# Transposes and first up parts of the first expert tile made inside the last attention iteration, and its first gelu part behind the squares of o

## The chip, the cores and the metric

One core of one Trainium2 chip. The metric is the device time of one execution in microseconds (us), lower is better. Engines: PE (TensorE, matmuls and their weight loads), VectorE (DVE in rows), ScalarE (ACT), GpSimd (POOL), and SyncE (SP), which only issues DMAs. The first four each run their own program in order; they meet at semaphores.

## The reference

A transformer layer in two halves, on x of 8 x 512 tokens by 256, f32.

```python
x = x + attention(layernorm(x))      # delta-rule linear attention, 4 heads, keys 128, values 64
x = x + experts(layernorm(x))        # top 2 of 8 experts, hidden 1024, exact gelu

# attention, for each token in order
pred = k_t^T S;  S = S + k_t (beta_t * (v_t - pred))^T;  o_t = q_t^T S
o = o * rsqrt(mean(o * o) + eps) * norm_w * silu(g);  return o @ Wo
# experts
out += w[:, eid] * (gelu(x @ w1[eid].T) @ w2[eid].T)
```

## The kernel before

The 4096 tokens are 32 tiles of 128 (T = 32). The **attention stage** is a software pipeline: in each iteration `i` of each engine's loop stand steps of several tiles in different states (PE `first_w(i - 3)`, `wo_make(i - 4)`, `xn2T_make(i - 5)`). The recurrence over a tile is solved as a triangular system: an inverse made in 7 levels (`y_make`, `x_make`), then `first_w`, `residual_make` and `corrected_w`, then the output (`out_state`, `out_chunk`). PE runs this loop for T + 3 iterations (L1483 to L1519). ScalarE and VectorE have their last iterations written out by hand, L1059 to L1136 and L2277 to L2359. The order of all work is that of the program text of each engine; no planner is at work.

A tile's last steps are a serial path over the engines: `out_chunk` (PE, L1392), `o_square` (ScalarE, L912, four squares with sums), `o_scale` (VectorE), `o_rsqrt` (GpSimd, L681), `o_norm` (VectorE, L1860), `oT_make` (PE, L1402), `oT_evac` (ScalarE) and `oT_low` (VectorE), `wo_make` (PE, L1416), `attention_residual` and `ln2_stats` (VectorE, L1869, L1876), `ln2_scale` (GpSimd, L628), `ln2` (ScalarE, L799), `xn2T_make` (PE, L1434), `xn2T_evac` (ScalarE, L929), `logits_make` (PE, L1448), `logits_copy` (ScalarE, L936), then the routing on VectorE (`best_logit` and what follows, every four tiles), ranks on PE (`rank`), and scattering of the rows into a table in HBM by GpSimd (`scatter`). Tokens of one expert stand together in that table.

In the same way a tile's W is made: `first_w` (PE, L1324), `first_w_evac` (ScalarE, L887), `residual_make` (PE, L1338), `residual` (VectorE, L1824), `corrected_w` (PE, L1356), `w_evac` (ScalarE, L895), `out_chunk`.

The **expert stage** takes 36 tiles of up to 256 rows, each belonging to one expert (8 of them to two). Tile 0 holds rows of the first 20 attention tiles, so it can be loaded while the last attention tiles are still worked on: SyncE's `load_rows(0, 0)` (L559, L569) reads 256 rows as soon as the table of experts is made. Steps of an expert tile: `xT_make` transposes its rows in four f32 transposes (PE, L1521, in rows L1533); `xT_hi` copies them to f16 (ScalarE, L1038) and `xT_lo` makes the rest that f16 leaves out (VectorE, L2228, in rows L2230); `up` (PE, L1557) makes hidden rows in 8 parts m of 6 matmuls each (products with high and low parts), raising `s_hps` after every second m; `hidden` (ScalarE, L1045) makes a gelu over two parts and its f16 copy; `hidden_lo` (VectorE, L2232) the low part of it; `down` (PE, L1577) the output product; `rows_out` and `accumulate` add the rows to the output. Every call of `up` reads the number of the expert into a register. ScalarE needs another table for gelu than for the functions of the attention stage; it is loaded by an instruction of its own that the compiler sets ahead of the gelu (a row ACT_TABLE_LOAD).

Matmuls of f16 stand in rows as L1158, copies on ScalarE as L789 and most small VectorE steps as L1901, since helpers make them; they are told apart by tile names. W is `first_w_evac`'s result, W_s `w_evac`'s, rho the residual's, rowA the normalised rows, w_hi and w_lo the up weights, w_s the down weights, osq the squares and o.

Around the change, PE before: last loop iteration (i = 34) with `wo_make(30)`, `rank(27)`, `first_w(31)`, `out_state(31)`, `residual_make(31)`, `corrected_w(31)`; then L1598 to L1632: `xT_make(0, 0)`, `out_chunk(31)`, `xn2T_make(30)`, `up(0, 0)` m 0 and 1, `logits_make(30)`, `up` m 2 and 3, `xT_make(0, 1)`, `oT_make(31)`, `up` m 4 and 5, `wo_make(31)`, and so on to `down(0, 0)`. ScalarE before (L1114 to L1130): `x_evac(31, 6)`, `first_w_evac(31)`, `late_hi(4)`, `late_hi(5)`, `w_evac(31)`, `ln2(30)`, `xT_hi(0, 0)`, `o_square(31)`, `xn2T_evac(30)`, `logits_copy(30)`, `late_hi(6)`, `xT_hi(0, 1)`, `oT_evac(31)`, `hidden` part 0. VectorE before (L2310 to L2331): `first_gate(27)`, `attention_residual(30)`, `ln2_stats(30)`, `residual(31)`, four routing steps, `xT_lo(0, 0)`, `o_scale(31)`, `o_norm(31)`.

Of the kernel before, what the change touches and what calls it, by code (L numbers as in the profile page):

```python
# [8 lines left out]
T = B * N // P  # L9
# [36 lines left out]
EARLY = 2 * T - LATE  # L46
# [25 lines left out]
def build(nc, x, wq, wk, wvg, wb, wo, norm_w, router, w1, w2, eye, fconst, iconst, out):  # L72
# [3 lines left out]
    with ctx:  # L76
# [210 lines left out]
        s_whi = sem("w_hi_ready")  # L287
# [499 lines left out]
        def _(act):  # L787
# [79 lines left out]
            def x_evac(n, lev):  # L867
                if not 0 <= n < T:
                    return
                q = n % 2  # L870
                done(act, s_xps[q], n // 2, 6, lev)
                if lev == LEVELS - 1:
                    evac(odd(XT[:, n % RING, :, :], lev), packed(p_xt[q], lev)).then_inc(s_xup[q], 1)
                    return
                evac(changed(n % RING, lev), PS[q][:, :].rearrange("p (w n s) -> p w n s", w=2, s=1 << lev)).then_inc(s_xup[q], 1)
# [11 lines left out]
            def first_w_evac(n):  # L887
                if not 0 <= n < T:
                    return

                done(act, s_zps, n - 1)
                done(act, s_wps, n)
                evac(W0[:, :, :], p_p).then_inc(s_ws, 1)
# [18 lines left out]
            def o_square(n):  # L912
                if not 0 <= n < T:
                    return
                done(act, s_oTp, n - 1)
                done(act, s_oarg, n - 1)
                done(act, s_ops, n)
                for h in range(H):
                    act.activation(osq[:, h, :], p_o[:, h, :], ACT.Square, scale=1.0 / O_SCALE,
                                   accum_out=osum[:, h:h + 1]).then_inc(s_osq, 1)  # L920
# [8 lines left out]
            def xn2T_evac(n):  # L929
                if not 0 <= n < T:  # L930
                    return
                done(act, s_lgps, n - 1)
                done(act, s_xn2Tp, n)
                evac(xn2T[:, :, :].rearrange("p k n -> p (k n)"), p_xn2T).then_inc(s_xn2Ts, 1)
# [103 lines left out]
            def xT_hi(i, q):  # L1038
                act.wait_ge(s_gTp, i * 4 + (q + 1))

                if not (isinstance(i, int) and i * 4 + q < 2):
                    act.wait_ge(s_hps, i * 16 + 4 * (q - 1))
                evac(xTh[:, q % 2, :, :], p_gT).then_inc(s_gTh, 1)

            def hidden(i, q, ms=range(4)):  # L1045
                for m in ms:
                    act.wait_ge(s_hps, i * 16 + (4 * q + m + 1))

                    if not (isinstance(i, int) and i * 4 + q < 1):
                        act.wait_ge(s_hlo, i * 16 + (4 * (q - 1) + m + 1))  # L1050
                    if m == 0 and not (isinstance(i, int) and i * 4 + q < 2):
                        act.wait_ge(s_yops, i * 4 + (q - 1))
                    n = halves(i, q) * P
                    gelu = hf[:, m, :].rearrange("p (m n) -> p m n", m=2)[:, :, 0:n]
                    act.activation(gelu, p_h[m].rearrange("p (m n) -> p m n", m=2)[:, :, 0:n], ACT.Gelu, scale=1.0 / W_SCALE).then_inc(s_gelu, 1)  # L1055
                    act.wait_ge(s_gelu, i * 16 + (4 * q + m + 1))
                    evac(hhi[:, q % 2, 2 * m:2 * m + 2, 0:n], gelu, H_SCALE).then_inc(s_hhi, 1)
# [54 lines left out]
            logits_copy(T - 3)  # L1112
            oT_evac(T - 2)
            x_evac(T - 1, 6)  # L1114
            first_w_evac(T - 1)
            late_hi(4)
            late_hi(5)

            w_evac(T - 1)
            ln2(T - 2)  # L1120
            xT_hi(0, 0)
            o_square(T - 1)
            xn2T_evac(T - 2)
            logits_copy(T - 2)
            late_hi(6)
            xT_hi(0, 1)
            oT_evac(T - 1)
            hidden(0, 0, range(0, 1))
            late_hi(7)
            hidden(0, 0, range(1, 2))  # L1130

# [24 lines left out]
        def _(pe):  # L1156
# [105 lines left out]
            def gram(n, a):  # L1262
                if not 0 <= n < T:
                    return
                for s in (s_kTs, s_kTl, s_qs, s_ql):
                    done(pe, s, n)

                if a == 1:
                    reach(pe, s_pos, Ranked.n)
                done(pe, s_AT, n - 1)  # L1270
                for h in range(2):
                    hh = [KQ[:, n % RING, part, 2 * a + h, :, :] for part in range(2)]
                    last = product(p_gram[a][:, h, :, :], [x[:, 0, :] for x in hh], hh)
                last.then_inc(s_gram, 1)
# [205 lines left out]
                Ranked.n = n // C + 1  # L1480

            pe.wait_ge(s_ident, 16)
            for i in range(T + 3):  # L1483
                gram(i - 2, 0)
                gram(i - 2, 1)
                out_chunk(i - 4)
                y_make(i - 3, 5)
                k_proj(i - 1, 0)
                xn2T_make(i - 5)
                y_make(i - 2, 0)  # L1490
                state_make(i - 4)
                x_make(i - 3, 5)
                y_make(i - 2, 1)
                logits_make(i - 5)
                k_proj(i - 1, 1)
                x_make(i - 2, 1)
                y_make(i - 3, 6)
                oT_make(i - 4)
                q_proj(i - 1, 0)
                y_make(i - 2, 2)  # L1500
                q_proj(i - 1, 1)
                beta_proj(i - 1)
                x_make(i - 3, 6)
                x_make(i - 2, 2)
                p_make(i - 2)
                wo_make(i - 4)
                y_make(i - 2, 3)
                rank(i - 7)
                first_w(i - 3)
                out_state(i - 3)  # L1510
                x_make(i - 2, 3)
                xnT_make(i)
                residual_make(i - 3)
                k_transposes(i - 1)
                y_make(i - 2, 4)
                vg_proj(i - 1, 0)
                vg_proj(i - 1, 1)
                corrected_w(i - 3)
                x_make(i - 2, 4)  # L1519

            def xT_make(i, q):  # L1521
                if isinstance(i, int):
                    i, q = divmod(i * 4 + q, 4)
# [71 lines left out]
                if KH - 1 in ms:  # L1595
                    last.then_inc(s_yops, 1)

            pe.wait_ge(s_xup[0], 6 * T // 2)  # L1598
            xT_make(0, 0)
            out_chunk(T - 1)  # L1600
            xn2T_make(T - 2)
            pe.wait_ge(s_tab, 1)
            pe.wait_ge(s_whi, EARLY)
            pe.wait_ge(s_wlo, EARLY)
            pe.wait_ge(s_xup[1], 6 * T // 2)
            up(0, 0, range(0, 2))
            logits_make(T - 2)
            done(pe, s_gs, T - 1)
            done(pe, s_th, T - 1)
# [72 lines left out]
        def _(dve):  # L1682
# [545 lines left out]
            def xT_lo(i, q):  # L2228
                dve.wait_ge(s_gTh, i * 4 + (q + 1))
                dve.tensor_tensor(xTl[:, q % 2, :, :], p_gT, xTh[:, q % 2, :, :], ALU.subtract).then_inc(s_gTl, 1)  # L2230
# [84 lines left out]
            oT_low(T - 2)  # L2315
            second_gate(T - 5)
            first_gate(T - 5)
            attention_residual(T - 2)
            ln2_stats(T - 2)
            residual(T - 1)  # L2320
# [2 lines left out]
            slot_sums(T - 5)  # L2323
            slots(T - 5)

            dve.wait_ge(s_xg[0], 16)
            xT_lo(0, 0)
            o_scale(T - 1)
            o_norm(T - 1)
            xT_lo(0, 1)  # L2330
# [118 lines left out]
```

## Time and profile before

| | |
|---|---|
| median of 3 runs | 910.33 us (907.74 to 911.69) |
| profiled execution, its own time | 914.49 us |
| its span | 912.7 us |
| PE busy | 850.3 us (93%) |
| VectorE, ScalarE, GpSimd busy | 625.5, 596.5, 439.3 us |
| mean granted PE clock | 0.978 of full |
| transition between the stages | about 480 to 512 us |

Times of rows are us from the start of the span. In a row of a timeline stand start, duration, engine, line, operation, output<-input, count, and in brackets the engine's idle time before it with what ended it. In a row of stretches stand, for each engine, the busy time and (in brackets) the count, then the granted clock of PE (1.00 is 2.4 GHz, 0.50 is 1.2 GHz), the share of the DMA engines at work, and GB/s. Consecutive matmuls overlap, so a duration is longer than the distance to the next start.

### The profile page before, as it was taken

Reading aid. Unit: us, or ns where it says so; the run is one execution under the profiler, and the core shown is the slowest. Engines: PE = TensorE matmul, PEld = TensorE weight load, DVE = VectorE, ACT = ScalarE, POOL = GpSimd, SP = SyncE. Lnnn points to the kernel's source line nnn. Section 1 sums busy time; section 2 is a strip of 40 time slices with the busy share of each in tenths; the row PEclk is TensorE's granted clock in tenths of the full one; section 3 lists DMA queues with packets and bytes.
Section 4 is the critical chain, followed back from the end, with each engine's and each line's share of the span. In section 5 each row is a group of like instructions: output and inputs, shape, how many; then the busy total and the mean of one; then the engine's idle time right before and its main releaser. Section 6 shows DMA issues by size and latency. Waiting matters only on the chain.

```text
span 912.7 us, 29508 instructions
## 1 busy us (share of the span) xinstructions
PE 850.3 (93%) x9870; PEld 669.4 (73%) x9871; DVE 625.5 (69%) x1832; ACT 596.5 (65%) x1645; POOL 439.3 (48%) x430
## 2 busy tenths in 40 slices
PE   3799999999999999999988979999999999999995
PEld 2578887788877888778876657777777777777773
DVE  4678898898988989888885755544455554455552
ACT  3478887888888888888766725444446544444551
POOL 2155554767677676676646543332223222222333
PEclk8999999999999999999997989999999999999998
DMA  6022222333233332332233252322233332223223
GB/s 225 2 71 66 82 65 77 95 95 106 84 95 99 90 107 83 97 99 82 84 107 88 72 118 48 48 48 48 43 48 66 50 50 46 46 46 46 47 36 34
DMA packets 50652, 67.14 MB, mean 74 GB/s; under 512 B 6464, under 2 KB 35008, under 8 KB 50528
## 3 DMA queue, kind: packets, MB, share of 16 engines
q1 hardware_dynamic: 36640, 46.46, 17.5%
q0 software_dynamic: 13344, 17.97, 11.5%
q8 instruction: 79, 1.29, 0.6%
q10 hardware_dynamic: 544, 1.05, 0.3%
q14 instruction: 45, 0.37, 0.1%
HBM read 41.84 MB, written 23.61 MB: 72 GB/s over the span
## 4 chain that ended last, share of the span: by engine, by line
PE 77%; issue 7%; ACT 4%; DVE 4%; POOL 4%; DMA 3%; SPq 0%; DVEq 0%; ACTq 0%; POOLq 0%
PE ps L1158 71%; DMA wst<-w 2%; PE ps L1247 2%; PE ps L1533 2%; ACT inverse_levels L789 1%; PE ps L1190 1%; PE ps L1413 1%; POOL kscale L616 1%; DVE inverse_levels L1815 1%; DMA wb_in<-wb 1%; POOL out L769 1%; POOL w_lo L665 0%; PE ps L1445 0%; ACT kq_wvg L844 0%; ACT Lh L789 0%
## 5 line engine op out<-in xcount | busy, mean ns | idle before, releaser
L789 ACT ACTIVATE inverse_levels<-ps 128x512 f16<-128x512 f32 (+1 forms) x324 | 163.0, 520 | 147.9 <-PE ps L1533 120.6
L769 POOL DMA_INDIRECT out<-inverse_levels,yidx x71 | 119.6, 1684 | 256.2 <-DVE inverse_levels L2273 194.6
L1158 PE MATMUL ps<-inverse_levels,w_hi 128*128 128x256 f16 (+1 forms) x1376 | 192.9, 255 | 1.9 <-issue 1.3
L2236 DVE SCALAR_TENSOR_TENSOR KpAT<-kq_wvg,inverse_levels 128x512 f16<-128x512 f32 (+1 forms) x144 | 98.5, 687 | 111.9 <-ACT inverse_levels L789 109.2
L1158 PE MATMUL ps<-inverse_levels,w_lo 128*128 128x256 f16 (+1 forms) x688 | 164.2, 255 | 0.0
L1158 PE MATMUL ps<-w_s,inverse_levels 128*128 x426 | 141.9, 379 | 6.5 <-issue 3.3
L1158 PEld LDWEIGHTS ps<-inverse_levels,w_hi 128*128 x1376 | 125.4, 98 | 15.7 <-issue 3.2
L1055 ACT ACTIVATE kq_wvg<-ps 128x512 f32<-128x512 f32 (+1 forms) x144 | 85.0, 590 | 67.0 <-PE ps L1158 51.1
L1158 PE MATMUL ps<-w_s,KpAT 128*128 x426 | 116.1, 273 | 1.0 <-issue 1.0
L789 ACT ACTIVATE inverse_levels<-kq_wvg 128x512 f16<-128x512 f32 (+1 forms) x144 | 89.8, 624 | 4.6
L1815 DVE CAST_PREDICATED inverse_levels<-mask_s,ps 128x256 f16<-128x256 int8 x192 | 82.1, 428 | 15.0 <-PE ps L1158 10.0
L616 POOL TENSOR_TENSOR kscale<-karg,fc 128x8 f32<-128x8 f32 x32 | 52.7, 1647 | 81.6 <-DVE karg L1745 81.6
L1158 PEld LDWEIGHTS ps<-w_s,inverse_levels 128*128 128x128 f16 x426 | 41.6, 98 | 53.9 <-issue 10.0
L1158 PE MATMUL ps<-wqk,inverse_levels 128*128 128x512 f16 (+1 forms) x263 | 78.1, 384 | 2.8 <-DVE inverse_levels L1714 2.3
L1158 PE MATMUL ps<-inverse_levels 128*128 128x64 f16 x1408 | 68.8, 193 | 9.3 <-DVE inverse_levels L1815 9.1
L2269 DVE TENSOR_SCALAR inverse_levels<-ps,gate 128x256 f32<-128x256 f32 x69 | 30.3, 479 | 68.8 <-PE ps L1158 68.5
L694 POOL DMA_INDIRECT routed_rows<-rowA,slot x64 | 67.7, 1057 | 18.4 <-issue 12.4
L1158 PE MATMUL ps<-kq_wvg,inverse_levels 128*128 128x512 f16 (+1 forms) x263 | 73.5, 387 | 1.8 <-issue 1.8
L1158 PEld LDWEIGHTS ps<-inverse_levels 128*128 128x128 f16 x1408 | 55.8, 99 | 22.1 <-DVE inverse_levels L1815 13.6
L1158 PE MATMUL ps<-inverse_levels,Lh 128*128 128x64 f16 x896 | 64.2, 194 | 8.3 <-ACT inverse_levels L789 4.6
L1158 PEld LDWEIGHTS ps<-inverse_levels,w_lo 128*128 x688 | 67.6, 98 | 5.5
L1158 PEld LDWEIGHTS ps<-inverse_levels,Lh 128*128 128x128 f16 x896 | 47.2, 100 | 20.2 <-ACT inverse_levels L789 10.7
(239 smaller groups left out, 1920.7 us busy)
## 6 DMA issues: line engine op xcount, KB each, us to landing
wst<-w SPq DMA_DIRECT2D x58, 256.0 KB, 2.8
inverse_levels<-eye SPq DMA_DIRECT2D x35, 256.0 KB, 5.2
x_s<-x SPq DMA_DIRECT2D x32, 128.0 KB
out<-x_s SPq DMA_DIRECT2D x32, 128.0 KB, 1.7
x_s<-routed_rows SPq DMA_DIRECT2D x7, 260.0 KB
Lh<-routed_rows SPq DMA_DIRECT2D x7, 260.0 KB
Vp<-routed_rows SPq DMA_DIRECT2D x7, 260.0 KB
rowA<-routed_rows SPq DMA_DIRECT2D x7, 260.0 KB
```

The source lines that it names most:

```text
L616: return pool.tensor_tensor(dst, src, half_neg[:, 0:n], ALU.pow)
L694: pool.indirect_dma_start(out=routed, out_offset=bass.IndirectOffsetOnAxis(ap=slot[:, g % 2, k, c:c + 1], axis=0), in_=rowA[:, g % RG * C ...
L769: pool.indirect_dma_start(out=out, out_offset=bass.IndirectOffsetOnAxis(ap=yidx[:, q, a:a + 1], axis=0), in_=yrow[:, q % 2, a, :], in_offs ...
L789: return act.activation(dst, src, ACT.Copy, scale=scale)
L1055: act.activation(gelu, p_h[m].rearrange("p (m n) -> p m n", m=2)[:, :, 0:n], ACT.Gelu, scale=1.0 / W_SCALE).then_inc(s_gelu, 1)
L1158: return pe.matmul(dst, lhsT, rhs, start=start, stop=stop, **kw)
L1190: last = pe.transpose(p_xnT[:, k * P:(k + 1) * P], xn[:, k * P:(k + 1) * P], ident)
L1247: last = pe.transpose(p_kT[:, h, :], Kp[:, n % RING, h, :], ident)
L1533: last = pe.transpose(p_gT[:, k, a * P:(a + 1) * P], xg[q % 4][:, a, k * P:(k + 1) * P], ident)
L1815: dve.copy_predicated(even(Y[:, lev - 1, :, :], lev), level_mask(lev, 0, H), packed(p_y[q], lev)).then_inc(s_ys[q], 1)
L2236: dve.scalar_tensor_tensor(hlo[:, q % 2, two, 0:n], hf[:, m, :].rearrange("p (m n) -> p m n", m=2)[:, :, 0:n], H_SCALE, hhi[:, q % 2, two, ...
L2269: step(dve.tensor_scalar(yrow[:, par, a, :], p_yo[a][:, 0, :], gate[:, par, a:a + 1], None, ALU.mult))
```

## The change

On PE `xT_make(0, 0)` and the first two up parts of tile 0 move from behind the loop into its last iteration (i = T + 2 = 34): the transposes go ahead of `first_w(31)`, part m = 0 ahead of `out_state(31)`, part m = 1 behind `residual_make(31)`. The waits of these steps move with them. The definitions of `xT_make`, `expert_of`, `load_experts`, `parts_of`, `up` and `down` move above the loop, unchanged. On ScalarE `xT_hi(0, 0)` moves ahead of `first_w_evac(31)`, and part 0 of the gelu of tile 0 (`hidden(0, 0, range(0, 1))`) moves right behind `o_square(31)`, ahead of `xn2T_evac(30)`. On VectorE `xT_lo(0, 0)` moves ahead of `attention_residual(30)`.

```diff
@@ ScalarE
             x_evac(T - 1, 6)
+            xT_hi(0, 0)
             first_w_evac(T - 1)
             late_hi(4)
             late_hi(5)
 
             w_evac(T - 1)
             ln2(T - 2)
-            xT_hi(0, 0)
             o_square(T - 1)
+            hidden(0, 0, range(0, 1))
             xn2T_evac(T - 2)
             logits_copy(T - 2)
             late_hi(6)
             xT_hi(0, 1)
             oT_evac(T - 1)
-            hidden(0, 0, range(0, 1))
             late_hi(7)
             hidden(0, 0, range(1, 2))
@@ PE, in the loop
                 rank(i - 7)
+                if i == T + 2:
+                    pe.wait_ge(s_xup[0], 6 * T // 2)
+                    xT_make(0, 0)
                 first_w(i - 3)
+                if i == T + 2:
+                    pe.wait_ge(s_tab, 1)
+                    pe.wait_ge(s_whi, EARLY)
+                    pe.wait_ge(s_wlo, EARLY)
+                    pe.wait_ge(s_xup[1], 6 * T // 2)
+                    up(0, 0, range(0, 1))
                 out_state(i - 3)
                 x_make(i - 2, 3)
                 xnT_make(i)
                 residual_make(i - 3)
+                if i == T + 2:
+                    up(0, 0, range(1, 2))
                 k_transposes(i - 1)
@@ PE, behind the loop
-            pe.wait_ge(s_xup[0], 6 * T // 2)
-            xT_make(0, 0)
             out_chunk(T - 1)
             xn2T_make(T - 2)
-            pe.wait_ge(s_tab, 1)
-            pe.wait_ge(s_whi, EARLY)
-            pe.wait_ge(s_wlo, EARLY)
-            pe.wait_ge(s_xup[1], 6 * T // 2)
-            up(0, 0, range(0, 2))
             logits_make(T - 2)
@@ VectorE
             second_gate(T - 5)
             first_gate(T - 5)
+            dve.wait_ge(s_xg[0], 16)
+            xT_lo(0, 0)
             attention_residual(T - 2)
             ln2_stats(T - 2)
             residual(T - 1)
...
             slots(T - 5)
 
-            dve.wait_ge(s_xg[0], 16)
-            xT_lo(0, 0)
             o_scale(T - 1)
```

## Rows read from the trace of the kernel before

**Rows 1.** Busy time by stretch: stretch, its length, engines, granted clock, DMA share, GB/s

```profile
473.60:477.00 3.40, 3.19 (x42) 2.82 (x43) 1.72 (x8) 1.01 (x3) 0.00 (x0) 0.51 0.28 108
477.00:480.40 3.40, 1.88 (x46) 1.52 (x44) 3.13 (x16) 2.57 (x6) 2.18 (x4) 0.99 0.02 5
480.40:490.60 10.20, 8.44 (x82) 6.90 (x79) 5.73 (x25) 5.53 (x20) 5.29 (x6) 0.51 0.24 65
490.60:494.00 3.40, 2.59 (x31) 2.05 (x28) 2.31 (x7) 3.00 (x8) 3.09 (x5) 0.98 0.30 74
...
486.50:487.50 1.00, 0.27 (x5) 0.11 (x3) 0.43 (x2) 0.66 (x2) 0.72 (x1) 0.50 0.00 0
700.00:880.00 180.00, 180.00 (x1398) 137.45 (x1397) 94.06 (x215) 91.41 (x151) 56.83 (x34) 1.00 0.31 48
```

**Rows 2.** Chain of work that ended last, in the transition

```profile
499.81 1.28 ACT L1055
...
507.99 0.19 ACT logits L789
```

**Rows 3.** Timeline of PE

```profile
487.64 1.44 PE L1158 MATMUL ps<-wo_s,inverse_levels 128*128 128x256 f16 x6 [0.87 <-DVE inverse_levels L1721]
...
489.13 0.37 PE L1158 MATMUL ps<-R,inverse_levels 128*128 128x64 f16 x4
489.32 0.83 PE L1158 MATMUL ps<-S_s,kq_wvg 128*128 128x64 f16 x12
490.24 0.21 PE L1158 MATMUL ps<-W,Lh 128*128 128x64 f16 x1
...
491.64 0.19 PE L1158 MATMUL ps<-rho,inverse_levels 128*128 128x64 f16 x1 [0.67 <-DVE rho L1829]
...
491.93 0.63 PE L1533 MATMUL ps<-fc,x_s 128*128 128x128 f32 x4
492.63 1.08 PE L1158 MATMUL ps<-W_s,KpAT 128*128 128x64 f32 x8
...
494.56 0.39 PE L1158 MATMUL ps<-inverse_levels,w_hi 128*128 128x256 f16 x2 [0.62 <-DVE inverse_levels L2230]
...
495.87 0.56 PE L1158 MATMUL ps<-router_s,inverse_levels 128*128 128x8 f32 x4
...
498.73 0.38 PE L1413 MATMUL ps<-fc,osq 128*128 128x128 f32 x2
...
512.22 0.39 PE L1158 MATMUL ps<-w_s,inverse_levels 128*128 x1 [0.72 <-DVE KpAT L2236]
...
534.65 1.06 PE L1533 MATMUL ps<-fc,x_s 128*128 128x128 f32 x4
```

**Rows 4.** Timeline of ScalarE

```profile
489.61 0.38 ACT L789 ACTIVATE W<-ps 128x256 f16<-128x256 f32 x1 [2.29 <-PE ps L1158]
...
492.93 0.59 ACT L789 ACTIVATE inverse_levels<-ps 128x512 f16<-128x512 f32 x1
493.83 0.22 ACT L919 ACTIVATE osq<-ps 128x64 f32<-128x64 f32 x1 [0.32 <-PE ps L1158]
...
494.63 0.40 ACT L789 ACTIVATE inverse_levels<-ps 128x256 f32<-128x256 f32 x1
...
499.81 1.28 ACT L1055 ACT_TABLE_LOAD   x1
...
502.28 0.61 ACT L789 ACTIVATE kq_wvg<-wst 128x512 f16<-128x512 f32 x1
```

**Rows 5.** Timeline of VectorE

```profile
491.07 0.42 DVE L1829 SCALAR_TENSOR_TENSOR rho<-Vp,ps 128x256 f16<-128x256 f32 x1 [0.67 <-PE ps L1158]
...
493.61 0.69 DVE L2230 TENSOR_TENSOR inverse_levels<-ps,inverse_levels 128x512 f16<-128x512 f32 x1 [0.49 <-ACT inverse_levels L789]
...
496.18 0.86 DVE L1865 SCALAR_TENSOR_TENSOR osq<-ps,ors,gs 128x64 f32<-128x64 f32 x4 [1.15 <-POOL ors L616]
```

**Rows 6.** Timeline of SyncE: the row load of expert tile 0

```profile
483.21 0.41 SPq L559 DMA_DIRECT2D x_s<-routed_rows  x1
```

More of the change, by code:

```diff
@@ L1482, in _ @@
             pe.wait_ge(s_ident, 16)
[L1483 to L1519, printed above, removed]
             def xT_make(i, q):
@@ L1596, in down @@
                     last.then_inc(s_yops, 1)
-            pe.wait_ge(s_xup[0], 6 * T // 2)
-            xT_make(0, 0)
+            for i in range(T + 3):
+                gram(i - 2, 0)
+                gram(i - 2, 1)
+                out_chunk(i - 4)
+                y_make(i - 3, 5)
+                k_proj(i - 1, 0)
+                xn2T_make(i - 5)
+                y_make(i - 2, 0)
+                state_make(i - 4)
+                x_make(i - 3, 5)
+                y_make(i - 2, 1)
+                logits_make(i - 5)
+                k_proj(i - 1, 1)
+                x_make(i - 2, 1)
+                y_make(i - 3, 6)
+                oT_make(i - 4)
+                q_proj(i - 1, 0)
+                y_make(i - 2, 2)
+                q_proj(i - 1, 1)
+                beta_proj(i - 1)
+                x_make(i - 3, 6)
+                x_make(i - 2, 2)
+                p_make(i - 2)
+                wo_make(i - 4)
+                y_make(i - 2, 3)
+                rank(i - 7)
+                if i == T + 2:
+                    pe.wait_ge(s_xup[0], 6 * T // 2)
+                    xT_make(0, 0)
+                first_w(i - 3)
+                if i == T + 2:
[4 more added lines that the diff above has]
+                    up(0, 0, range(0, 1))
+                out_state(i - 3)
+                x_make(i - 2, 3)
+                xnT_make(i)
+                residual_make(i - 3)
+                if i == T + 2:
+                    up(0, 0, range(1, 2))
+                k_transposes(i - 1)
+                y_make(i - 2, 4)
+                vg_proj(i - 1, 0)
+                vg_proj(i - 1, 1)
+                corrected_w(i - 3)
+                x_make(i - 2, 4)
             out_chunk(T - 1)
             xn2T_make(T - 2)
-            pe.wait_ge(s_tab, 1)
-            pe.wait_ge(s_whi, EARLY)
-            pe.wait_ge(s_wlo, EARLY)
-            pe.wait_ge(s_xup[1], 6 * T // 2)
-            up(0, 0, range(0, 2))
             logits_make(T - 2)
```

## The prediction

> **What bounds the kernel now.** I read the stretches first. From 700 to 880 us PE is busy 180.00 of 180.00 us at full clock [rows 1]: the expert stage is PE from end to end, and whatever makes PE late at its start stays to the end. So the change is judged by how late PE leaves the transition. In the same view the reader is to see how sparse PE work and the granted clock go together there: level 0.51 from 473.6 to 477.0, then 0.99 with PE busy 1.88 of 3.40 us, then 0.51 from 480.4 to 490.6, then 0.98.
>
> The chain of waits comes next [rows 2]. It runs through ScalarE's table load at 499.81 and through the logits copy at 507.99. So in the transition the end is set by the last tile's serial path (squares of o, o, its transposes, the output product, layernorm, router), not by PE work alone. That path leads on to `down(0, 0)`, which waits 0.72 us for a low part that VectorE makes behind the routing of the last tile at 512.22 [rows 3]. I find no slack behind the last router product into which a delay could go.
>
> Then the engines in order of time. PE [rows 3]: output product of tile 30 at 487.64, first W of tile 31 at 489.13, `out_state` 489.32, residual 490.24, corrected W 491.64 (0.67 us idle in front), the four transposes 491.93, the last `out_chunk` 492.63, the first up part at 494.56 (0.62 idle in front), router product of tile 30 at 495.87. So PE's idle time that the change could fill is about 1.3 us before 495.87. ScalarE [rows 4] and VectorE [rows 5] show how each answers.
>
> **The change, step by step.** Nothing is added to the sum of work but one reading of the expert's number; the rest moves.
>
> Row load. It is issued at 483.21 [rows 6] and no DMA is at work from 486.5 to 487.5 [rows 1], so the rows are there before PE asks at 489.1. SyncE's queue is unchanged, but its second row load waits for the residual product, some 2.5 us later; the first 2.5 us of up parts in front of the second transposes cover it. Cost 0; without the cover up to 2.5.
>
> Transposes (`xT_make(0, 0)`, four of f32). They go ahead of `first_w`, at 489.1, where the clock is still low: 1.06 us at that level (534.65) against 0.63 at full (491.93) [rows 3]. They end at 490.2, and first W starts 0.9 us later than 489.13.
>
> High and low part. Before, from the end of the transposes (492.56) the high part started at 492.93 behind other ScalarE work, took 0.59 [rows 4], the low part started 493.61 and took 0.69 [rows 5], and PE went on at 494.56. Without the queue on ScalarE that is 0.59 + 0.09 + 0.69 + 0.26, 1.7 us with the hand-over: the first up part can start at 491.9. PE has only first W (0.2 us) until then, so it idles about 1.4 us, **a new wait**. Behind it in program order stand `out_state`, the residual product and the corrected W, which in rows 3 were already under way at 489.32.
>
> VectorE is blocked too: `xT_lo(0, 0)` stands ahead of `attention_residual(T - 2)`, which could run at 489.1 (487.64 + 1.44 [rows 3]) and now runs at 491.6. With it go `ln2_stats`, GpSimd's scale and all that GpSimd has queued behind, the rsqrt for the last o among them: o's norm moves from 496.18 [rows 5] to about 498.7, ending at 499.5. That proves to be covered below.
>
> First up part: m = 0 and 1 took 494.56 to 495.87, so 0.65 us each. It runs to 492.55. `out_state` took 0.92 us at the low level (489.32 to 490.24), 0.46 at full; the residual as much; with 0.2 of latency the residual on VectorE starts at 493.65 instead of 491.07. The second part runs 493.45 to 494.1 beside it. Residual to corrected W was 0.57 us [rows 3, 5]: corrected W at 494.2, **2.55 us later** than 491.64. The extra register reading I bound by nothing and by the 0.62 us of the idle time at 494.56; I take 0, since VectorE's step covers it.
>
> Corrected W to `out_chunk` was 0.99 us, `out_chunk` to the last square 2.0 us (492.63 to 494.63 [rows 3, 4]): `out_chunk` at 495.2, squares done 497.2.
>
> The gelu. It now stands right behind the squares and ahead of `xn2T_evac(T - 2)`. Table load, gelu and high part held ScalarE from 499.81 to 502.28, 2.47 us [rows 4]. So `xn2T_evac` starts at 499.7 and PE's router product of tile 30 follows 0.5 us later, at 500.2. Before, the up parts stood between the transposes of tile 30 and that product and hid its wait; now nothing does: PE, done with `out_chunk` and two transposes at about 496.6, **waits some 3.6 us**. Router product 500.2 against 495.87: **4.3 us later**. Everything that follows on PE up to `oT_make(T - 1)` (498.73, now 503.0) is unchanged work in unchanged order; o's norm (499.5) is ready. ScalarE no longer has to make the first gelu at 499.81, but the path from o's transposes through the output product, VectorE, GpSimd and ScalarE is serial and does not go through it; I take its saving as 0, bounded by 2.47.
>
> On this load row and rule differ. The gelu's table load takes 1.28 us and starts 0.01 us after the evacuation before it, and the whole piece with gelu and high part is over in 2.47 [rows 4]. The Trainium skill (ScalarE: Activation LUTs, What ACT_TABLE_LOAD costs) adds a drain of about 1.38 us to the load for every switch; by that page 4.3 would be 5.7, an estimate. The rows show no such drain and the sum goes by them.
>
> Clock. Two gaps, 1.4 us at 490.4 and 3.6 us at 496.6, stand where there were 0.67 and 0.62. A stretch with PE busy 1.88 of 3.40 us was followed by the low level [rows 1], and the stretch from 496.6 to 500.2 is emptier. Before, the level was 0.98 from 490.6. If it falls behind the gap, the up parts, transposes and products from 500.2 on run at half speed for as long as it stays low. The shortest low stretch in rows 1 is 3.4 us, which costs up to 1.7 us of work; a long one like 480.4 to 490.6 up to 5. Some of it lies in the wait itself. Ends: 0 and 3.4; I take 1.2, nearer the short stretch.
>
> Sum: 4.3 + 1.2 = **+5.5 us**. The profiled execution took 914.49 us (span 912.7), 4.2 over the median of 910.33; the sum is a difference, so 914.49 becomes 920.0 and the median 915.8. About 0.5% (4.55 us) is what a measurement of this kernel can tell from no change.
>
> **The rivals.** *Stall without a clock fall, or partly made up.* The waits are as above but the clock stays or its low stretch lies in the wait, and ScalarE's lighter load gives back up to 1 or 2 us. +1.5 to +4.5, 912 to 915. For it: 490.6 to 494.0 had PE busy only 2.59 of 3.40 at 0.98 and stayed high. Against: the gap of 3.6 us is longer than any PE wait of rows 3. Chance 0.27.
>
> *The clock stays low already at 490.6.* What ended the low stretch there was f16 work: output product, first W, `out_state`, residual [rows 1, 3]. Transposes and an idle 1.4 us take the place of half of it. If it stays low to 494.0, the two up parts and the products between run at half speed, about +1.1 us, then `out_chunk`, about as much, on top of 5.5: +6.5 to +9.5, 917 to 920. Chance 0.12. The Trainium skill (TensorE: Matmul & The Clock Gate, PE-mode transpose) says that transposes do not count as PE work for the full clock; by that rule this rival gains. No row shows transposes alone against the clock.
>
> *Not slower.* The mechanism is the one that fills gaps. ScalarE's 2.47 us of load and gelu leave the chain at 499.81 [rows 2, 4], and the up parts fill 0.67 and 0.62 of PE's waits [rows 3]. If the transposed rows came early enough, the gain would be 1.3 up to 3.8 us: 906.5 to 909. It decides at the point where the low part is ready by 490.3, when the residual product would not be held; that needs the transposes to end before 488.6, and PE's output product alone ends at 489.1. It also needs the evacuation of tile 30 not to stand behind the gelu, and it does. Chance 0.11, with 0.03 for over 0.5%.
>
> **How the numbers follow.** Forecast case 0.50, stall alone 0.27, low clock from 490.6 on 0.12, not slower 0.11. Slower by over 0.5%: 0.43 of the forecast case, 0.03 of the stall alone, all 0.12: 0.58. Faster: 0.03. Same: 0.39. The likeliest gives 915.8. The range takes in most of the stall alone and the clock rival, and a little of the last, for medians of few runs that spread from 907.74 to 911.69: 909.5 to 920.
>
> **What would show it.** In the profile after: transposes near 489.1 ahead of first W; PE idle over 1 us ahead of the first up part, its releaser the low part on VectorE; corrected W some 2.5 us later against the output product of tile 30; the table load right behind the squares; PE idle over 3 us ahead of the router product of tile 30, its releaser the evacuation on ScalarE; a low level of the clock after it. I am wrong if the router product comes less than 2 us later, if its wait is not there, or if `down(0, 0)` has made good what the router product lost.

## The result and the profile after

The kernel after takes 915.48 us, the median of 6 runs (914.17 to 917.45), against 909.01 (907.22 to 911.69) for 6 runs of the kernel before beside it. The ratio is 1.0083, with a 95% interval of 1.0062 to 1.0104: slower by 5.6 to 9.5 us. The medians are 6.5 us apart; forecast were 5.5. Three single executions of variants below took 1072 to 1398 us at a mean granted clock of 0.56 to 0.75 and are left out of their ratios.

The two profiled spans (912.7 before, 915.6 after) can't be subtracted. The output product of tile 30, the last step of PE ahead of everything that moved, starts at 487.64 before and at 491.35 after, and before loses some 8 us in a stall behind `down(0, 0)` that both kernels show (last section). So I count from that output product to `down(0, 0)`, on PE (from unrounded starts, so a figure can differ by 0.01 from the rows):

| us behind the output product of tile 30 | before | after | fill_both (below) |
|---|---|---|---|
| transposes of tile 0 | 4.29 | 1.49 | 1.49 |
| first up part | 6.91 | 4.26 | 4.30 |
| corrected W of tile 31 | 4.00 | 8.06 | 6.79 |
| router product of tile 30 | 8.23 | 14.17 | 12.90 |
| transposes of o, tile 31 | 11.08 | 18.45 | 15.72 |
| `down(0, 0)` | 24.58 | 31.93 | 29.16 |

Timeline of PE, after; it answers to [rows 3]:

```profile
491.35 1.44 PE L1158 MATMUL ps<-wo_s,inverse_levels 128*128 128x256 f16 x6 [0.87 <-DVE inverse_levels L1725]
...
492.84 1.09 PE L1495 MATMUL ps<-fc,x_s 128*128 128x128 f32 x4
493.72 0.42 PE L1158 MATMUL ps<-R,inverse_levels 128*128 128x64 f16 x4
495.61 0.61 PE L1158 MATMUL ps<-inverse_levels,w_hi 128*128 128x256 f16 x2 [1.47 <-DVE inverse_levels L2234]
...
496.86 0.85 PE L1158 MATMUL ps<-S_s,kq_wvg 128*128 128x64 f16 x12
...
498.16 0.61 PE L1158 MATMUL ps<-inverse_levels,w_hi 128*128 128x256 f16 x2
...
499.40 0.19 PE L1158 MATMUL ps<-rho,inverse_levels 128*128 128x64 f16 x1
...
500.40 1.08 PE L1158 MATMUL ps<-W_s,KpAT 128*128 128x64 f32 x8 [0.60 <-issue]
...
505.51 0.99 PE L1158 MATMUL ps<-router_s,inverse_levels 128*128 128x8 f32 x4 [3.81 <-ACT inverse_levels L789]
...
509.80 0.38 PE L1413 MATMUL ps<-fc,osq 128*128 128x128 f32 x2
...
523.28 0.39 PE L1158 MATMUL ps<-w_s,inverse_levels 128*128 x1 [0.93 <-ACT inverse_levels L789]
```

The transposes (L1495 here) stand ahead of first W, and PE idles 1.47 us in front of the first up part, released by the low part on VectorE. `out_state`, at 489.32 in [rows 3], starts at 496.86 behind it. No wait stands in front of corrected W at 499.40: it follows the second up part (498.16 to 499.40), which at the low level ends later than the residual on VectorE (498.46 + 0.42). The second wait is 3.81 us in front of the router product, released by ScalarE.

Timeline of ScalarE, after; it answers to [rows 4]:

```profile
493.97 0.60 ACT L789 ACTIVATE inverse_levels<-ps 128x512 f16<-128x512 f32 x1 [2.95 <-PE ps L1495]
...
502.31 0.22 ACT L919 ACTIVATION_READ_ACCUMULATOR osq<-ps 128x1 f32 x1
502.54 1.28 ACT L1055 ACT_TABLE_LOAD   x1
503.84 0.60 ACT L1055 ACTIVATE kq_wvg<-ps 128x512 f32<-128x512 f32 x1
504.47 0.63 ACT L789 ACTIVATE inverse_levels<-kq_wvg 128x512 f16<-128x512 f32 x1
505.00 0.37 ACT L789 ACTIVATE inverse_levels<-ps 128x256 f32<-128x256 f32 x1
```

The table load begins as the squares end (502.31 + 0.22), and the evacuation for which PE waits is the row at 505.00, behind the load, the gelu and its copy: 2.46 us.

Timeline of VectorE, after; it answers to [rows 5]:

```profile
494.67 0.69 DVE L2234 TENSOR_TENSOR inverse_levels<-ps,inverse_levels 128x512 f16<-128x512 f32 x1 [3.12 <-ACT inverse_levels L789]
495.27 0.41 DVE L1878 SCALAR_TENSOR_TENSOR x_s<-ps,x_s 128x256 f32<-128x256 f32 x1
...
498.46 0.42 DVE L1833 SCALAR_TENSOR_TENSOR rho<-Vp,ps 128x256 f16<-128x256 f32 x1 [1.90 <-PE ps L1158]
```

VectorE idles 3.12 us for the high part, then adds the residual to tile 30, whose product had ended at 492.79; the residual of tile 31 starts 7.11 us behind the output product, 3.43 before (491.07 - 487.64).

Busy time by stretch, after; it answers to [rows 1], with its columns:

```profile
485.80:499.30 13.50, 10.37 (x88) 8.00 (x88) 6.30 (x29) 6.83 (x22) 6.84 (x9) 0.50 0.17 50
...
499.30:502.70 3.40, 1.80 (x20) 1.43 (x18) 1.85 (x4) 1.96 (x11) 1.79 (x2) 0.99 0.57 129
502.70:509.50 6.80, 3.91 (x18) 3.13 (x19) 0.95 (x5) 3.86 (x7) 5.39 (x5) 0.51 0.39 131
...
700.00:880.00 180.00, 180.00 (x1390) 136.58 (x1389) 93.51 (x218) 88.79 (x146) 55.44 (x33) 1.00 0.31 49
```

The level is 0.50 until 499.3 and again from 502.7 to 509.5, where [rows 1] have 0.98 from 490.6 on. In the expert stage PE is busy 180.00 of 180.00 us at full clock in both, so what `down(0, 0)` lost stays lost (stalls like the one of the last section apart).

### The profile page after: what moved, and what is told of

The parts are those of the page before. It is cut to its first block, busy times and chain, and to the rows that moved or that the text cites. A ratio compares the mean times of both kernels' runs of the same rounds, so it can differ in the third digit from the quotient of the medians.

```text
span 915.6 us, 29511 instructions
## 1 busy us (share of the span) xinstructions
PE 854.2 (93%) x9870; PEld 671.9 (73%) x9871; DVE 628.9 (69%) x1832; ACT 596.5 (65%) x1645; POOL 442.7 (48%) x430
## 4 chain that ended last, share of the span: by engine, by line
PE 56%; POOL 8%; issue 6%; DMA 4%; DVE 4%; ACT 4%; DVEq 0%; POOLq 0%; ACTq 0%
PE ps L1158 52%; DMA wst<-w 4%; PE ps L1495 2%; POOL kscale L616 2%; POOL w_lo L665 1%; POOL Ll L679 1%; ACT inverse_levels L789 1%; POOL w_s L665 1%; POOL ors L616 1%; PE ps L1247 1%; POOL routed_rows L694 1%; DVE inverse_levels L1819 1%; DVE nL L1778 1%; POOL rs L616 1%; PE ps L1413 1%
```

## The experiments

The stretch from the output product to `down(0, 0)` is read from one profile each; the ratio, over 5 to 12 executions, is to the kernel before on the same chip. Two profiles of after differ by 1.36 us in the stretch, so where stretch and ratio disagree the ratio counts.

| kernel | corrected W | router product | `down(0, 0)` | ratio [95%] |
|---|---|---|---|---|
| before | 4.00 | 8.23 | 24.58 | 1 |
| after | 8.06 | 14.17 | 31.93 | 1.0083 [1.0062, 1.0104] |
| gelu_back | 8.07 | 11.72 | 30.69 | 1.0051 [1.0032, 1.0070] |
| gelu_alone | 4.07 | 10.18 | 26.45 | 1.0036 [1.0020, 1.0051] |
| up_back | 5.70 | 13.52 | 31.59 | 1.0050 [1.0031, 1.0068] |
| gelu_behind_evac | 4.10 | 9.12 | 25.41 | 1.0001 [0.9982, 1.0019] |
| transposes_alone | 5.70 | 11.60 | 27.39 | 1.0027 [1.0009, 1.0045] |
| low_later | 8.07 | 14.29 | 32.13 | 1.0082 [1.0050, 1.0114] |
| fill | 8.07 | 14.38 | 32.27 | 1.0069 [1.0049, 1.0090] |
| between | 4.09 | 10.45 | 27.06 | 1.0027 [1.0005, 1.0048] |
| before_again | 4.07 | 9.25 | 24.93 | one execution |
| after_again | 8.08 | 15.29 | 33.29 | one execution |
| fill_both | 6.79 | 12.90 | 29.16 | 1.0033 [1.0015, 1.0051] |
| before_fill | 3.83 | 8.08 | 24.27 | 0.9983 [0.9966, 1.0000] |

**gelu_back**: after, with the gelu back behind `oT_evac(T - 1)`.

```diff
             o_square(T - 1)
-            hidden(0, 0, range(0, 1))
...
             oT_evac(T - 1)
+            hidden(0, 0, range(0, 1))
```

> The changed kernel with the first gelu part back in its old place behind the evacuation of o's transposes; the rest of the change stays. Measure: from the start of the output product of tile 30 to the start of down(0, 0), 24.58 us in the kernel before and 31.93 in the changed one, and PE's wait ahead of the router product of tile 30, 3.81 us in the changed one. My theory (table load, gelu and high part, 2.47 us, stand in front of the evacuation that this product waits for): the wait falls to about 1.3 us, the stretch to 28 to 29.5 us, the time to 3 to 4.5 us over the kernel before. Rival (the up parts and transposes in the loop do it all, the gelu fills idle time of ScalarE): wait and stretch stay near 3.8 and 32 us, the time stays 6.5 us over.

Timeline of PE and stretches, gelu_back:

```profile
503.88 0.99 PE L1158 MATMUL ps<-router_s,inverse_levels 128*128 128x8 f32 x4 [1.24 <-ACT inverse_levels L789]
```
```profile
500.50:503.90 3.40, 1.56 (x18) 1.25 (x15) 1.64 (x2) 2.08 (x11) 1.50 (x3) 0.99 0.71 161
503.90:510.70 6.80, 6.80 (x32) 5.46 (x33) 1.88 (x6) 3.46 (x7) 5.31 (x5) 0.50 0.36 115
```

The wait shrinks from 3.81 to 1.24 us and the router product comes 2.45 us earlier, as expected; `down(0, 0)` only 1.24, so the stretch of 30.69 misses the 28 to 29.5 that I expected. The low level came all the same, and now it lies on 6.80 us in which PE is busy throughout, where in after it covered a wait. By the ratios the gelu's place costs some 0.3%, 3 us; the intervals of the two overlap, so this run alone does not show it.

**gelu_alone**: before, with only the gelu moved behind the squares.

```diff
             o_square(T - 1)
+            hidden(0, 0, range(0, 1))
             xn2T_evac(T - 2)
...
             oT_evac(T - 1)
-            hidden(0, 0, range(0, 1))
```

> The kernel before with one move alone: the first gelu part right behind the squares of o. My theory: the up parts still stand ahead of the router product and cover a part, the evacuation comes 2.5 us later, the router product 1.7 us later than 495.87, stretch 26.3 us, up to 27.8 if the clock falls, time 1.5 to 3 us over the kernel before. Rival (the move shortens ScalarE's chain by 2.47 us and PE has cover): stretch 22 to 24.6, time 0 to 2.5 us under.

Timeline of PE and stretches, gelu_alone:

```profile
497.21 0.58 PE L1158 MATMUL ps<-router_s,inverse_levels 128*128 128x8 f32 x4 [1.71 <-ACT inverse_levels L789]
```
```profile
493.90:497.30 3.40, 1.57 (x13) 1.18 (x14) 1.02 (x5) 3.10 (x8) 2.98 (x4) 1.00 0.72 225
```

With the up parts in their old place the wait is 1.71 us instead of 3.81, and from corrected W to the router product it is 6.11 us instead of 4.23: the gelu costs 1.88. `down(0, 0)` comes 1.87 later, so nothing is given back behind it. The ratio, 1.0036 [1.0020, 1.0051], shows that the gelu's move alone costs time, some 3.3 us, a little more than expected. The level stays full through the wait, with PE busy 1.57 of 3.40 us; in gelu_back the row at 500.5 has 1.56 of 3.40, and the low level follows.

**up_back**: after, with both up parts back behind `xn2T_make(T - 2)`.

```diff
                 first_w(i - 3)
-                    up(0, 0, range(0, 1))
...
                 residual_make(i - 3)
-                    up(0, 0, range(1, 2))
...
             xn2T_make(T - 2)
+            up(0, 0, range(0, 2))
```

> The changed kernel with the two up parts back behind the transposes of tile 30, transposes of the expert tile, its high and low part and the gelu as changed. My theory: no PE wait for the low part in the loop, but the residual on VectorE still stands behind the low part, the attention residual and the layernorm sums, so the corrected W is about 1.9 us late; the gelu then holds the router product to about 3.6 us late: stretch 28 to 30 us, time 3.5 to 5.5 us over the kernel before. Rival (the wait of the up parts inside the loop is the whole loss): stretch 24.6 to 26, time within 1 us of before.

Corrected W is now 1.70 us late instead of 4.06; that rest I put down to VectorE's wait for the high part, behind which the residual stands. The profile misses the expectation: 31.59, since its clock stayed low until 19.4 us behind the output product. The ratio, from many executions, puts the up parts' share at 0.3%, 3 us, with intervals that just overlap.

**transposes_alone**: up_back with the gelu back too, so only the transposes with their high and low parts stand early.

```diff
@@ the edit of up_back, and
             o_square(T - 1)
-            hidden(0, 0, range(0, 1))
...
             oT_evac(T - 1)
+            hidden(0, 0, range(0, 1))
```

> The changed kernel with both up parts back behind the transposes of tile 30 and the gelu back in its old place: only the transposes of the expert tile with their high and low part stay early. Stretch as before (24.58 us before, 31.94 changed). My theory: the low part on VectorE still holds the last residual, corrected W 1.7 us late as with the up parts back alone, router product of tile 30 about 2 us late, stretch 26.5 to 28 us depending on the clock, time 2 to 3.5 us over before. Rival (the early transposes cost only their place on PE, 0.9 us): stretch 25 to 25.8, time under 1.5 us over.

27.39 and 1.0027 [1.0009, 1.0045], as expected: even this part alone costs. In its profile the clock was low until 12.0 us behind the output product.

**gelu_behind_evac**: before, with the gelu right behind the evacuation that PE waits for.

```diff
             xn2T_evac(T - 2)
+            hidden(0, 0, range(0, 1))
...
             oT_evac(T - 1)
-            hidden(0, 0, range(0, 1))
```

> The kernel before with the first gelu part moved one step less far: behind the evacuation of tile 30's transposes, where ScalarE sits idle 1.50 us. My theory: it delays only the logits copy and the late weight split; the serial path goes through GpSimd with 0.15 us to spare, so stretch 24.2 to 24.9 us and time within 1 us of before. Rival (ScalarE's table load at 499.81 bounds the path): stretch near 22.1, time 2.5 us under.

Timeline of ScalarE, gelu_behind_evac:

```profile
497.27 0.40 ACT L789 ACTIVATE inverse_levels<-ps 128x256 f32<-128x256 f32 x1
497.69 1.28 ACT L1055 ACT_TABLE_LOAD   x1
```

One line lower the load costs nothing that can be measured, 1.0001 [0.9982, 1.0019], against 1.0036 for gelu_alone; the two intervals do not overlap. It wins nothing either, which rules out the rival. The profiled stretch of 25.41 misses the expected 24.2 to 24.9. Its clock was low until 8.2 us; before_again, low until 8.5, has 24.93. The other 0.5 us stand on ScalarE, as the rows around the evacuation of o's transposes show. First ScalarE before, then PE and ScalarE in gelu_behind_evac:

```profile
498.93 0.87 ACT L789 ACTIVATE inverse_levels<-ps 128x512 f16<-128x512 f32 x2 [1.16 <-PE ps L1533]
```
```profile
500.47 0.38 PE L1413 MATMUL ps<-fc,osq 128*128 128x128 f32 x2
```
```profile
501.25 0.86 ACT L789 ACTIVATE inverse_levels<-ps 128x512 f16<-128x512 f32 x2
```

The row of ScalarE (the high part of expert tile 1, then the evacuation of o) starts 0.20 us behind the transposes of o before (498.73 in [rows 3]) and 0.78 us here, without a wait: the logits copy and the weight splits that the gelu pushed back still stand in front of it.

**low_later**: after, with the low part on VectorE behind `ln2_stats(T - 2)`.

```diff
-            xT_lo(0, 0)
             attention_residual(T - 2)
             ln2_stats(T - 2)
+            xT_lo(0, 0)
             residual(T - 1)
```

> The changed kernel with the low part of the expert tile on VectorE behind the layernorm sums of tile 30 instead of ahead of its attention residual. My theory: the sums and GpSimd's scale come about 1.5 us earlier, but nothing waits for them, since the low part is bound by the high part on ScalarE all the same; stretch 31.5 to 32.2 us, time as the changed kernel, 5 to 7.5 us over before. Rival (the held attention residual and GpSimd's queue behind it carry part of the loss): stretch 30.5 or less.

32.13 and 1.0082: no change, as expected. GpSimd's scale starts 2.86 us behind the output product instead of 5.30, and nothing comes earlier for it: the layernorm of tile 30 and GpSimd's queue were covered.

**fill**: after, with 20 f16 products that nobody reads in the 3.81 us wait.

```diff
             xn2T_make(T - 2)
+            for _ in range(20):
+                mm(p_gT[:, 0, :], ones16[:, :], xTh[:, 0, 0, :])
             logits_make(T - 2)
```

> The changed kernel with 20 more matmuls (128x128 by 256 columns, f16, into the free buffer of the expert transposes, result unused) in PE's wait of 3.81 us ahead of the router product of tile 30. The low clock from 11.4 to 18.3 us behind the output product of tile 30 is what it tests. If that wait drops the clock: the clock stays full there, from the router product to o's transposes 2.9 us instead of 4.28, stretch 30 to 31 us, time 1 to 2 us under the changed kernel. Rival (the level follows something else, the f32 products or a grid that the work does not move): low stretch and 31.9 us stay.

Stretches, fill:

```profile
499.20:506.00 6.80, 4.25 (x38) 3.60 (x35) 2.35 (x6) 4.81 (x16) 4.50 (x5) 1.00 0.64 176
506.00:509.40 3.40, 3.21 (x16) 2.52 (x17) 0.00 (x0) 1.00 (x2) 2.15 (x2) 0.50 0.11 39
```

A miss: the second low stretch did not go away. It came 15.3 us behind the output product instead of 11.4 and lasted 3.4 us instead of 6.8, still over the work behind the router product, and `down(0, 0)` stands at 32.27. PE was busy 4.25 of the 6.80 us ahead of it. The ratio's interval overlaps that of after.

**between**: before, with the transposes between the residual product and corrected W, their high part behind `w_evac`, and the gelu behind the evacuation. It was meant as a version better than both.

```diff
                 residual_make(i - 3)
+                if i == T + 2:
+                    pe.wait_ge(s_xup[0], 6 * T // 2)
+                    xT_make(0, 0)
...
-            xT_make(0, 0)
             out_chunk(T - 1)
...
             w_evac(T - 1)
+            xT_hi(0, 0)
             ln2(T - 2)
-            xT_hi(0, 0)
             o_square(T - 1)
             xn2T_evac(T - 2)
+            hidden(0, 0, range(0, 1))
```

> A version meant to beat both: the kernel before with the four transposes between the residual product and the corrected W, where PE waits 0.67 us, the high part right behind the evacuation of W, and the gelu behind the evacuation of tile 30's transposes. My theory: the low part is ready 0.5 us earlier and takes away most of PE's wait of 0.62 us ahead of the first up part; corrected W at most 0.1 late; stretch 23.9 to 24.6 us at the clock of before (up to 25.4 at a longer low clock), time within 1 us of before, at best 0.6 under. Rival (transposes take the place of the residual's wait and then some): corrected W 0.5 late, stretch 25 or more.

A miss: 27.06 and 1.0027 [1.0005, 1.0048], slower than before. Corrected W keeps its time (4.09), and the low part is ready 0.5 us earlier than in gelu_behind_evac (6.50 against 7.02 us behind the output product, at the low level up to there in both). But the high part now stands ahead of `ln2(T - 2)` on ScalarE, which starts 0.5 us later (5.60 against 5.09), and the clock stayed low until 12.7: the router product comes at 10.45.

**before_again, after_again**: both kernels once more, unchanged, one execution each (918.52 and 924.02 us).

> The kernel before once more, for a second profile. It tells whether PE's loss of 6.35 us between down(0, 0) and the transposes of expert tile 4 (22.43 us there against 16.08 in the changed kernel), which the profile of before shows and no other, belongs to the kernel or to that one execution. If to the execution (mine): 16.1 us there and a span near 906 to 908. If to the kernel: 22.4 again. Low clock behind the output product of tile 30: until 3.1 us again if the level follows the work of this kernel, anything from 3 to 9 if it follows where the execution happens to stand.

> The changed kernel once more, for a second profile. Stretch from the output product of tile 30 to down(0, 0): 31.5 to 32.5 us if its clock levels follow its waits; down to 29.5 if the low stretches of the first profile were chance. 16.1 us from down(0, 0) to the transposes of tile 4.

Stretches, before_again, then after_again:

```profile
475.30:499.20 23.90, 19.67 (x195) 16.58 (x196) 14.70 (x58) 13.36 (x43) 11.65 (x13) 0.50 0.29 84
499.20:515.00 15.80, 14.24 (x126) 11.42 (x124) 8.47 (x28) 10.27 (x21) 12.65 (x13) 1.00 0.24 81
```
```profile
485.30:509.20 23.90, 16.48 (x113) 13.19 (x113) 7.57 (x27) 11.03 (x30) 12.51 (x13) 0.50 0.28 81
509.20:520.00 10.80, 9.66 (x82) 7.52 (x80) 6.46 (x19) 5.93 (x13) 6.07 (x7) 1.00 0.13 43
```

The same program gets low stretches of different length. Before, the level rose at 3.1 us behind the output product in one execution and at 8.5 in the other (499.20 - 490.73), at a cost of 0.35 us; after, it rose at 8.0 and fell again from 11.4 to 18.3 in one, and rose only at 20.4 in the other, and `down(0, 0)` moved from 31.93 to 33.29, past the 31.5 to 32.5 expected. Expected of both was also 16.1 us from `down(0, 0)` to the transposes of tile 4; the loss behind `down(0, 0)` came again, and in after_again too.

**fill_both**: after, with 6 f16 products ahead of the first up part and 34 in the second wait.

```diff
+                    done(pe, s_gs, T - 1)
+                    done(pe, s_th, T - 1)
+                    done(pe, s_kp, T - 1)
+                    for _ in range(6):
+                        mm(p_kv[:, 0:256], ones16[:, :], R16[:, :, :].rearrange("p h n -> p (h n)"))
                     up(0, 0, range(0, 1))
...
             xn2T_make(T - 2)
+            for _ in range(34):
+                mm(p_gT[:, 0, :], ones16[:, :], xTh[:, 0, 0, :])
             logits_make(T - 2)
```

> The changed kernel with PE's two waits filled: 6 more matmuls (128x128 by 256 columns, f16, result unused) ahead of the first up part, and 34 instead of 20 ahead of the router product of tile 30, about as long as that wait at full clock. If the waits are what holds or drops the clock: full clock from the second filler on, router product to o's transposes 2.9 us instead of 4.3, stretch from the output product of tile 30 to down(0, 0) 30 to 31 us if the first low stretch ends where it did, 29 if it ends sooner. Rival (the level does not follow PE's waits): low behind the router product again, stretch 31.9 us or more.

Timeline of PE and stretches, fill_both:

```profile
490.99 1.47 PE L1158 MATMUL ps<-R,ones 128*128 128x256 f16 x6
492.68 0.58 PE L1158 MATMUL ps<-inverse_levels,w_hi 128*128 128x256 f16 x2 [0.22 <-DVE inverse_levels L2241]
...
497.31 3.88 PE L1158 MATMUL ps<-inverse_levels,ones 128*128 128x256 f16 x34
501.28 0.58 PE L1158 MATMUL ps<-router_s,inverse_levels 128*128 128x8 f32 x4
```
```profile
493.10:497.00 3.90, 3.19 (x51) 2.87 (x50) 2.10 (x9) 1.72 (x4) 3.01 (x4) 1.00 0.20 39
497.00:510.00 13.00, 12.04 (x103) 9.63 (x101) 4.46 (x13) 8.27 (x22) 7.99 (x9) 1.00 0.33 103
```

Nothing of after's order is changed. The first up part still waits for the low part (4.30 us behind the output product, 4.26 in after), and from corrected W to the router product it is 6.11 us in both. What differs is the level: full from 493.1 on, 4.7 us behind the output product. `down(0, 0)` comes 2.77 us earlier, and the intervals of the ratios, 1.0015 to 1.0051 and 1.0062 to 1.0104, don't touch. The levels of one profile could be chance, as before_again and after_again show; the mean granted clock of all executions says that they are not: 0.981 to 0.986 in the 9 of fill_both, 0.974 to 0.978 in the 6 of after. This run separates the waits from the clock.

**before_fill**: before, with 25 such products in the last two loop iterations (5 ahead of `x_make(i - 3, 6)`, 3 ahead of `x_make(i - 2, 2)`, 5 ahead of `wo_make(30)`, and 6 ahead of `corrected_w` in both).

```diff
+            def filler(n):
...
+                for _ in range(n):
+                    mm(p_kv[:, 0:256], ones16[:, :], w1_hi[0][0][:, 0:256])
...
+                if i == T + 2:
+                    filler(5)
                 wo_make(i - 4)
...
+                if i >= T + 1:
+                    filler(6)
                 corrected_w(i - 3)
```

> The kernel before (no step moved) with 25 filler matmuls (f16, 256 columns, result unused) in PE's waits of its last two attention iterations: 5 and 3 ahead of the last inverse updates and 6 ahead of the corrected W in iteration 33, 5 ahead of the output product and 6 ahead of the corrected W in iteration 34. In both kernels the clock is low from about 7 us ahead of the output product of tile 30 to 3 to 8 us behind it. If f16 work in the waits keeps the clock full there, as in the changed kernel with both waits filled: no or a shorter low stretch, stretch to down(0, 0) 23.5 to 24.5 us, time 0.5 to 3 us under before. Rival (the waits there are not what drops it, the fillers only take PE's time): low stretch as before, time the same or up to 1.5 us over.

Stretches, before_fill:

```profile
476.30:486.40 10.10, 7.48 (x124) 6.13 (x121) 7.52 (x33) 7.38 (x23) 6.32 (x7) 1.00 0.14 33
486.40:489.90 3.50, 3.50 (x38) 2.67 (x37) 1.52 (x9) 0.80 (x3) 1.05 (x1) 0.51 0.32 109
489.90:510.00 20.10, 17.32 (x163) 13.81 (x161) 11.05 (x34) 15.03 (x37) 15.74 (x17) 1.00 0.29 91
```

The low stretch that in [rows 1] lasts 10.2 us (480.4 to 490.6) is 3.5 us long. The mean granted clock is 0.984 to 0.989 in its 12 executions, against 0.978 to 0.986 in the 17 of before beside them, so the products do hold the clock. The median is 906.48 us against 907.54; the interval reaches 1.0000, so a gain in time is likely but not shown.

## Why the prediction held, step by step

The direction, both new PE waits and the path were forecast. That 915.48 us came so close to the forecast 915.8 is luck: the kernel before measured 909.01 over 6 runs where the forecast started from 910.33, and that hides the 1.0 us by which the difference was too small.

**Row load, transposes, first wait.** As forecast. The rows were there; the transposes took 1.09 us at the low level (forecast 1.06), and PE idled 1.47 us (forecast 1.4) for the part that VectorE makes.

**Corrected W.** Forecast 2.55 us later; it is 4.06 in after and 2.79 in fill_both, where the level rises 4.7 us behind the output product. The step was right, but I let PE's work from 491.9 on run at full level. Also, I had the second up part end beside the residual on VectorE; at the low level it ended later and held corrected W itself.

**The gelu.** Forecast 3.6 us of wait, measured 3.81; its own part 1.8 (4.3 less 2.55), measured 1.88. The Trainium skill's drain (ScalarE: Activation LUTs, What ACT_TABLE_LOAD costs, about 1.38 us) did not appear: the load starts 0.01 us behind the squares and the piece takes 2.46.

**The rest of the path.** Taken as unchanged, with nothing given back, and so it is. From the transposes of o to `down(0, 0)` it is 13.50 us before, 13.48 after, 13.44 in fill_both. low_later bears out that what VectorE and GpSimd do later is covered.

**The clock** is the term that was mis-sized. I took 1.2 us between 0 and 3.4; it is 2.77, the difference of after and fill_both in the profiles, and 0.50%, some 4.5 us, in the ratios. 1.27 of the 2.77 lie ahead of corrected W, from a low stretch that did not end at 490.6 of before's time, and 1.50 behind it. The waits without this clock, fill_both against before, are 4.58 in the profiles and some 3.0 in the ratios, against my 4.3. The fairer pair is fill_both against before_fill, with products in the waits of both: 4.89 us, and 1.0050 as the quotient of the two ratios, some 4.5 us. So the 4.3 stands and the 1.2 was too small: what is left for the clock is 2.5 to 4.5 us, whichever pair is taken, and the runs do not settle it closer. (That 4.58 and 2.77 make 7.35 is no check: they are one difference cut in two.) I had the second fall and the longer first stretch as alternatives, the one in the forecast and the other in a rival of 0.12; both came.

**The rivals.** *Clock low already from 490.6* is the one that happened beside the forecast case: its +6.5 to +9.5 hold 7.35. That the change causes the longer first stretch is not shown: before_again has the low level until 8.5 without it, at a cost of 0.35 us. Whether transposes fail to raise the level, as the Trainium skill says (TensorE: Matmul & The Clock Gate, PE-mode transpose), no run here shows: the low stretch varies too much within one program. *Stall without a clock fall* is what fill_both makes on purpose: 1.0033, +3.0, inside its +1.5 to +4.5 (its profiled stretch, +4.58, just outside). *Not slower* decides at a low part ready by 490.3, that is 2.7 us behind the output product; it was ready at 4.0. gelu_behind_evac shows that even with the evacuation in front nothing is won from ScalarE's 2.47 us.

The parts add up in the ratios: transposes 0.27%, up parts 0.24% (gelu_back less transposes_alone), gelu 0.36%, together 0.87% against 0.83%. The transposes and the gelu are shown, each by an interval that stays above 1; the share of the up parts is a difference of two ratios whose intervals overlap, and rests on the profiles, where they move corrected W from 5.70 to 8.07.

## What to carry to other kernels

Pulling a step into an earlier idle gap pays only if its inputs come early enough; an in-order engine that waits for it holds everything behind it, and the place it leaves no longer covers the wait that it used to cover. A table load goes behind the evacuation that another engine waits for, not in front of it: one line of program was worth 3 us here. Two profiles are laid together at the last step that the change leaves alone, and where new PE waits appear, products that nobody reads show how much of the loss is waiting and how much is clock. One profile does not settle a clock effect of 1 to 3 us; the ratio and the mean granted clock of many executions say more.

## What was not expected of the hardware

**A stall** in 3 of 14 profiles (before, before_again, after_again), behind `down(0, 0)`. Timeline of PE, of ScalarE and of SyncE, before; the last fence is SyncE in after, without the stall:

```profile
528.31 0.27 PE L1158 MATMUL ps<-w_s,KpAT 128*128 x1 [1.05 <-issue]
528.42 0.38 PE L1158 MATMUL ps<-wqk,inverse_levels 128*128 x1
529.76 0.27 PE L1158 MATMUL ps<-wqk,KpAT 128*128 x1 [0.96 <-issue]
530.48 0.38 PE L1158 MATMUL ps<-wqk,inverse_levels 128*128 x1 [0.46 <-issue]
531.19 0.28 PE L1158 MATMUL ps<-wqk,KpAT 128*128 x1 [0.33 <-issue]
```
```profile
534.09 0.60 ACT L1055 ACTIVATE kq_wvg<-ps 128x512 f32<-128x512 f32 x1 [9.53 <-remote]
```
```profile
524.73 13.15 SPq L430 DMA_DIRECT2D routed_rows<-nL  x8
```
```profile
533.76 8.95 SPq L430 DMA_DIRECT2D routed_rows<-nL  x8
```

PE idles with "issue" between single products, ScalarE idles 9.53 us with a remote releaser, and SyncE's eight writes take 13.15 us instead of 8.95. From `down(0, 0)` to the transposes of tile 4 it is 22.43 us in before, 19.84 in before_again and 22.78 in after_again, instead of 16.09; to the transposes of tile 5 it is 35.21, 35.79 and 34.56 instead of 26.96, so the whole loss is 7.6 to 8.8 us. All three stalled profiles show the long writes (13.03 to 13.15, against 8.25 to 9.15 in the other eleven) and a low stretch of the clock behind, 6.8 us long. The kernel before stalled in both of its profiles and after in one of two; how often the executions behind the medians stalled is not known, and it bears on the 6.5 us between them. Nothing was tried against it; its cause is open.

**The clock's low stretch** differs between executions of one program: until 3.1 and until 8.5 us behind the output product in before; until 8.0 and once more from 11.4 to 18.3, or until 20.4 without a break, in after. And the same busy time was followed by either level (1.57 of 3.40 in gelu_alone, 1.56 in gelu_back). Which property of the work decides stays open; 20 filling products moved and shortened the second fall, 40 at two places removed it.
